# Moving the column-sum fold to VectorE and reordering four instruction queues of an attention kernel

## The reference, cut to what matters

```python
qkv = jnp.einsum('bsh,hf->bsf', x, w_qkv)             # split in q, k, v, 16 heads of 128
scores = jnp.einsum('bhqd,bhkd->bhqk', q, k) / jnp.sqrt(128.)
probs = jax.nn.softmax(scores, axis=-1)
values = jnp.einsum('bhqk,bhkd->bhkd', probs, v)      # k is kept, q is summed
out = jnp.einsum('bsf,fh->bsh', values, w_o)
x = _layernorm(x + out)
```

## Time and profile before

| | us |
|---|---|
| median of three runs | 2747.32 |
| the profiled execution, its own time | 2753.47 |
| its span, first to last instruction | 2751.7 |
| PE busy | 2644.6 (96%) |
| DVE busy | 2170.7 (79%) |
| ACT busy | 1562.8 (57%) |
| POOL busy | 1409.5 (51%) |

### The profile page before, as it was taken

One profiled execution on the slowest core, in us unless ns is written; L12 is line 12 of the kernel. 1 busy time (PEld: TensorE's weight loads), 2 busy tenths in 40 slices (PEclk: granted clock), 3 DMA queues, 4 the chain that ended last, 5 costly groups with the idle time before them and its releaser, 6 DMA issues.

```text
span 2751.7 us, 40658 instructions
## 1 busy us (share of the span) xinstructions
PE 2644.6 (96%) x12450; PEld 2163.3 (79%) x12450; DVE 2170.7 (79%) x3096; ACT 1562.8 (57%) x2627; POOL 1409.5 (51%) x1042
## 2 busy tenths in 40 slices
PE   9999999998999999989999999899999999999998
PEld 7777777777877777777777777777777778888887
DVE  6988888988788888878888888788888787433346
ACT  5655555557666666676556666666655532244434
POOL 3677767545655554556555545555555210266520
PEclk9999999999999999999999999999999999999999
DMA  5455455643533336344343453433334331378954
GB/s 176 146 168 154 150 168 151 220 159 114 181 114 116 112 112 209 110 136 151 107 123 111 121 192 113 168 108 103 104 117 145 101 119 42 107 237 249 260 151 153
DMA packets 351134, 397.51 MB, mean 144 GB/s; under 512 B 132780, under 2 KB 269996, under 8 KB 350496
## 3 DMA queue, kind: packets, MB, share of 16 engines
q1 hardware_dynamic: 340512, 383.92, 44.5%
q0 software_dynamic: 10496, 12.02, 2.4%
HBM read 299.58 MB, written 106.43 MB: 148 GB/s over the span
## 4 chain that ended last, share of the span: by engine, by line
PE 59%; DVE 7%; issue 6%; POOL 2%; ACT 1%; ACTq 0%; DVEq 0%; POOLq 0%
PE banks L2497 17%; PE banks L2568 13%; PE banks L2602 9%; PE banks L2406 5%; PE banks L2455 5%; PE banks L2468 3%; PE banks L2415 2%; DVE colsum L1918 2%; DVE neg_max L1901 1%; PE banks L2578 1%; PE banks L2442 1%; POOL val L948 1%; DVE rows_a L1948 1%; PE banks L2330 1%; POOL qk L957 0%
## 5 line engine op out<-in xcount | busy, mean ns | idle before, releaser
L2568 PE MATMUL banks<-qk 128*128 128x512 f32 x3072 | 786.0, 391 | 21.9 <-POOL qk L957 20.7
L1901 DVE TENSOR_REDUCE neg_max<-banks 128x1 f32<-128x1024 f32 x512 | 624.3, 1220 | 219.6 <-PE banks L2568 217.0
L2497 PE MATMUL banks<-xt,w_all 128*128 128x512 f32 x3024 | 761.4, 394 | 33.6 <-DVE rows_a L1948 12.0
L2497 PEld LDWEIGHTS banks<-xt,w_all 128*128 128x128 f32 x3024 | 565.7, 189 | 179.7 <-DVE rows_a L1948 22.2
L1413 ACT ACTIVATE raws<-banks,neg_max 128x1024 f32<-128x1024 f32 x392 | 438.4, 1118 | 459.8 <-DVE neg_max L1901 456.4
L2568 PEld LDWEIGHTS banks<-qk 128*128 128x128 f32 x3072 | 579.3, 189 | 147.0 <-POOL qk L957 23.3
L1918 DVE SCALAR_TENSOR_TENSOR colsum<-raws,inv,colsum 128x1024 f32<-128x1024 f32 x343 | 535.6, 1562 | 13.5
L2602 PE MATMUL banks<-wo_sb,val 128*128 128x512 f32 x1536 | 385.9, 396 | 16.0 <-POOL wo_sb L898 14.4
L2602 PEld LDWEIGHTS banks<-wo_sb,val 128*128 128x128 f32 x1536 | 292.2, 191 | 82.5 <-issue 19.0
L944 POOL TENSOR_TENSOR folded<-folded,colsum 64x1024 f32<-64x1024 f32 x49 | 116.9, 2385 | 376.3 <-ACT folded L1384 376.3
L2484 PE MATMUL banks<-xt,w_all 128*128 128x512 f32 x1152 | 279.4, 392 | 6.4 <-DVE xt L2117 6.4
(11 more groups left out here) (233 smaller groups left out, 3421.0 us busy)
## 6 DMA issues: line engine op xcount, KB each, us to landing
w_all<-w_jobs SPq DMA_DIRECT2D x144, 512.0 KB
w_all<-w_jobs SPq DMA_DIRECT2D x72, 768.0 KB
w_jobs<-xt SPq DMA_DIRECT2D x96, 256.0 KB, 3.5
x_jobs<-xt SPq DMA_DIRECT2D x48, 448.0 KB, 5.5
xt<-x_jobs SPq DMA_DIRECT2D x21, 1024.0 KB, 10.8
w_jobs<-w_all SPq DMA_DIRECT2D x72, 256.0 KB, 3.3
wo_raw<-in_w_o SPq DMA_DIRECT2D x63, 256.0 KB, 2.9
raws<-in_w_qkv SPq DMA_DIRECT2D x48, 256.0 KB
```

The costliest lines, as they stand in the source:

```text
L1901: dve.tensor_reduce(neg_max[:, t % 2], p_s[:, t % 2], AX_X, ALU.max, negate=True)\
L2497: ins = pe.matmul(psum[:, bank], w_slot[pos % 7][:, a, c], x[:, half, c], start=(opens and c == 0 and (a, half) == PASSES[0]), stop=(c == ...
L2568: ins = pe.matmul(p_s[:, t % 2, keys], qk[:, par, Q, a, at], qk[:, par, K, b, keys], start=((a, b) == PASSES[0]), stop=((a, b) == PASSES[-1]))
```

## The change

Six edits, none of which adds or removes arithmetic:

1. `fold_cs` of batches 1 to 3 goes from POOL to DVE, in step 1 right behind `max_tile`. POOL's semaphore for it disappears; `hi_cs` and the first `add_tile` of a head wait for DVE's.
2. POOL in batch 0: `lo_cs` stands ahead of `lo_t(n - 1, 1)`, and `lo_wo(n - 1, 1)` ahead of `sum_t(n, 0)`. SP in batch 0: in even slots `load_wo` comes right behind `store_w`.
3. POOL in the first halves: `scale_x` (k = 1) and `lo_x` (k = 0) go to the end of the half.
4. ACT: `copy_v` moves from step 7 to step 6; `evac_u` of P1 from step 1 to step 0 of the second halves of batches 1 to 3.
5. ACT, k = 1: the moments of tiles 0 and 1 of the second set are read later, tile 0 in step 7, tile 1 in step 0 of the second half, along with tile 2 and ahead of `write_x`.
6. PE: the product P3 of the second half is computed behind `spread` rather than ahead of it.

```diff
@@ -631,6 +631,8 @@
         def plain(i, s):
             n = 2 * i + s
             store_w(n + 1)
+            if s == 0 and i > 0:
+                load_wo(n - 1, n - 1, 1)
             if n + 2 < H:
                 load_w(n + 2, n + 2)
             if 2 <= n - 1 <= H - 3:
@@ -639,8 +641,6 @@
                 load_t(n, 0)
             if s == 1:
                 load_wo(n - 1, n - 1, 0)
-            elif i > 0:
-                load_wo(n - 1, n - 1, 1)
             x_step = n == 0 or (s == 1 and i < PB - 1)
             if x_step:
                 load_x(0, i + s, i + s)
@@ -939,10 +939,6 @@
             size = 7 * P if b < B - 1 else KC * P
             pool.tensor_tensor(low, x_own[:, 0:size], rounded(high), ALU.subtract).then_inc(pool_x, 1)
 
-        def fold_cs(m):
-            on_pool.wait_ge(act_cs, 3 * m + 1)
-            pool.tensor_tensor(folded[:], folded[:], colsum[0:HP], ALU.add).then_inc(pool_f, 1)
-
         def lo_val(m, r):
             on_pool.wait_ge(act_val, m + 1)
             pool.tensor_tensor(val2[:, r, LO], val[:, r], rounded(val2[:, r, HI]), ALU.subtract)\
@@ -990,18 +986,18 @@
             if s == 0 and not is_first(i):
                 lo_wo(n - 2, 0)
             late_sums = not isinstance(i, int) or 2 <= n - 1 <= H - 3
+            if not (is_first(i) and s == 0):
+                lo_cs(n - 1)
             if late_sums:
                 lo_t(n - 1, 1)
-            if not (is_first(i) and s == 0):
-                lo_cs(n - 1)
+            if s == 0 and not is_first(i):
+                lo_wo(n - 1, 1)
             if sums:
                 sum_t(n, 0)
             if not end:
                 lo_w(n + 2, Q)
             if x_step:
                 sum_x(0, i + s)
-            if s == 0 and not is_first(i):
-                lo_wo(n - 1, 1)
             if sums:
                 lo_t(n, 0)
             if not end:
@@ -1017,7 +1013,6 @@
             n = 2 * i
             m = n + 1
             at, k1 = k == 0, k == 1
-            fold_cs(n - 1)
             if at and b < B - 1:
                 sum_x(b, T * b)
             lo_cs(n - 1)
@@ -1026,14 +1021,14 @@
             lo_val(n - 2, 0)
             lo_block(m, 1, 1)
             add_v(i, 0)
-            if k1:
-                scale_x(2 * (b - 1))
             lo_val(n - 1, 1)
-            if at:
-                lo_x(b, T * b)
             lo_block(m, 1, 2)
             add_v(i, 1)
             lo_wo(n - 1, 1)
+            if k1:
+                scale_x(2 * (b - 1))
+            if at:
+                lo_x(b, T * b)
 
         def second_half(b, k, i):
             n = 2 * i + 1
@@ -1383,11 +1377,8 @@
             on_act.wait_ge(pool_cs, m)
             act.copy(folded[:], colsum[HP:P]).then_inc(act_cs, 1)
 
-        def hi_cs(m, by_pool=False):
-            if by_pool:
-                on_act.wait_ge(pool_f, m - (H - 3))
-            else:
-                on_act.wait_ge(dve_cs, m + 1)
+        def hi_cs(m):
+            on_act.wait_ge(dve_cs, m + 1)
             on_act.wait_ge(pe_cs, 2 * m)
             act.copy(cs[0:HP], folded[:]).then_inc(act_cs, 1)
@@ -1458,7 +1449,7 @@
                     if k1:
                         read_x(c, [0, 1])
                 if t == 2:
-                    hi_cs(n - 1, True)
+                    hi_cs(n - 1)
                     hi_upper_cs(n - 1)
                     if k1:
                         read_x(c, [2])
@@ -1471,7 +1462,6 @@
                     hi_val(n - 2, 0, i)
                     if k1:
                         read_x(c, [3])
-                        read_x(c + 1, [0])
                 if t == 5:
                     evac_v(i, 3)
                     hi_block(i, 0, m, 1, 1)
@@ -1483,10 +1473,9 @@
                     hi_block(i, 0, m, 1, 2)
                     hi_block(i, 0, m, 1, 3)
                     hi_wo(n - 1, 1, i)
-                if t == 7:
                     copy_v(i)
-                    if k1:
-                        read_x(c + 1, [1])
+                if t == 7 and k1:
+                    read_x(c + 1, [0])
                 exp_tile(n, t, ex_late)
 
         def second_half(b, k, i):
@@ -1496,13 +1485,17 @@
             c = 2 * (b - 1)
             for t in range(T):
                 if t == 0:
+                    if k1:
+                        read_x(c + 1, [1, 2])
+                    if b > 0:
+                        evac_u(i, AT_S1 + P1, m, 0)
                     upper_cs(n - 1)
                     if k1:
-                        read_x(c + 1, [2])
                         write_x(c, [0, 1])
                 if t == 1:
-                    evac_u(i, AT_S1 + P1, m, 0)
-                    if not (b == 0):
+                    if b == 0:
+                        evac_u(i, AT_S1 + P1, m, 0)
+                    else:
                         evac_v(i, 5)
                     if k1:
                         read_x(c + 1, [3])
@@ -1901,17 +1894,14 @@
             dve.tensor_reduce(neg_max[:, t % 2], p_s[:, t % 2], AX_X, ALU.max, negate=True)\
                 .then_inc(dve_m, 1)
 
-        def add_tile(n, t, of, by_pool=True):
+        def add_tile(n, t, of):
 
             tau = n * T + t
             on_dve.wait_ge(act_e, tau + 1)
             dve.reciprocal(inv[:, t % 2], rowsum[:, t % 2]).then_inc(dve_r, 1)
             on_dve.wait_ge(dve_r, tau + 1)
             if t == 0:
-                if by_pool:
-                    on_dve.wait_ge(pool_f, n - (H - 2))
-                else:
-                    on_dve.wait_ge(dve_cs, n)
+                on_dve.wait_ge(dve_cs, n)
                 dve.tensor_scalar(colsum[:], of[:, 0], inv[:, 0], None, ALU.mult).then_inc(dve_p, 1)
             else:
                 on_dve.wait_ge(dve_p, tau)
@@ -2016,7 +2006,7 @@
                     if t == 5:
                         lo_val(n - 1, 1)
                 if t >= 1:
-                    add_tile(n, t - 1, ex, False)
+                    add_tile(n, t - 1, ex)
 
         def first_half(b, i):
             n = 2 * i
@@ -2037,6 +2027,8 @@
                 if t == 5:
                     add_block(i, 0, m, 2)
                 max_tile(n, t)
+                if t == 1:
+                    fold_cs(n - 1)
                 if t == 3:
                     times_v(0 if eighth else b, n - 1, 1, i - 1)
                 if t == 4:
@@ -2578,7 +2573,7 @@
                 pe.matmul(p_o[:, half], ones[:], cs[:, at], start=True, stop=True).then_inc(pe_cs, 1)
 
         def spread_last():
-            on_pe.wait_ge(dve_cs, H - 1)
+            on_pe.wait_ge(dve_cs, M)
             for half in range(HALVES):
                 at = slice(half * NB, half * NB + NB)
                 for part, of in ((HI, cs[:]), (LO, last_lo)):
@@ -2648,7 +2643,7 @@
             of = b + 1 if end else b
             for t in range(T):
                 scores(n, 1, t, True)
-                for j in {0: (P1, P2), 1: (P7, P6), 2: (P4, P5), 3: (P3,)}.get(t, ()):
+                for j in {0: (P1, P2), 1: (P7, P6), 2: (P4, P5)}.get(t, ()):
                     qk_unit(of, i, 1, j)
                 if t == SPREAD:
                     if seventh:
@@ -2657,6 +2652,7 @@
                         on_pe.wait_ge(act_ve, evacs(i, 6))
                     on_pe.wait_ge(dve_qc, 3 * (2 * i + 2 - H) + 1)
                     spread(n - 1)
+                    qk_unit(of, i, 1, P3)
                 if t in (4, 5):
                     v_early(of, i, t - 4)
                 if t >= 4:
```

2 lines of the change are left out of this document (1 added, 1 removed).

## The result

The changed kernel takes 2769.97 us, the median of five runs (2767.57 to 2778.45), the kernel before 2750.27 in five runs beside it (2746.57 to 2754.33). The ratio is 1.0068, its 95% interval 1.0054 to 1.0083. The forecast was 2743 with a range of 2712 to 2765. The spans of the two profiled executions are 2768.3 and 2751.7 us.

What follows compares the result with a forecast made beforehand. The PE, busy 96% of the span, was taken as the bound, with batch 0 pairs set by the weight sums' chain. Terms +19.1 - 24.9 - 2.6 + 3.8 = -4.6 gave 2743 us from the median, range 2712 to 2765.

Steps and rivals of the forecast that it cites:

- The chain: Batch 0: the weight sums' four links, not the PE, set the pair's 73.94 us; lengthened, heads 2 to 14 lose +19.1.
- its new link of 23.2 us: Batch 0, last link of a pair: with lo_cs ahead of lo_t it takes 23.2 us, against 16.2.
- rival A: Batch 0: the chain has slack, pairs fall towards 69.0 us; 2690 to 2725, chance 0.24.
- The 1.8 us between 72.2 and 73.94: Batch 0: difference between the four summed links and the measured pair, said to be the PE's own stalls.
- POOL loses twice that, nobody waits for it there: Middle pairs of batches 1 to 3: DVE gets 2.4 us more a pair, POOL loses twice that, without anyone waiting.
- the -0.85 us for each odd slot: Odd middle slots, 17 of them: gaps at P6 and P3 go, with other small waits; -14.5 us in all.
- The signs that the prediction named: In middle pairs no PE gap at P6 and none at copy_v, pairs of about 63 us.
- Rival C: Odd middle slots: DVE's fold becomes the bound at 1848 ns, the gain of 14.5 us goes; 2757, chance 0.07.
- k = 1 and k = 0: First and second halves of these pairs: k = 1 -22.6 and +20.0 us, k = 0 -4.4 and +8.2 us.
- The 40.7 us for the half: k = 1 second half: write_x waits for scale_x, delaying exponentials and P4; +6.7 us each, three times +20.0.
- Rival B: Chain at 78.2 us a pair, k = 1 second half +9, middle pairs winning only 10.4; 2753 to 2770, chance 0.21.
- Rival D: Whole kernel: only an order changes, gains and losses both small; 2747, no change, chance 0.10.

Runs made afterwards that it cites:

- The odd swap alone: Kernel before with one edit: POOL in odd slots of batch 0 does lo_cs ahead of lo_t(n - 1, 1); 2784.08 us, ratio 1.0111.
- its undoing: Changed kernel with POOL in odd slots of batch 0 doing lo_t(n - 1, 1) ahead of lo_cs again; 2738.47 us, ratio 0.9954.
- the last kernel: Changed kernel, lo_t before lo_cs (odd slots), add_v after lo_cs, units before store, load_t before store_t, k = 1 scale_x early, ACT work spread; 2687.67 us.

## Why the prediction was wrong

**Batch 0 was right in its mechanism, and its size is in part luck.** The chain, its new link of 23.2 us (23.8 measured in the pair that it was read from, 24.4 on average), the shorter third link (13.3, measured 13.2), the pair of 77.2 (77.3), and where the PE would wait instead: for exponentials behind `hi_t`. The odd swap alone and its undoing show the cause from both sides. The last link came out 1.2 us above its forecast on average, and the first shrank by 1.1, which was not forecast; the two cancel. And the argument against rival A, that the links add up to the measured pair, was empty, because they always do. The 1.8 us between 72.2 and 73.94 are not the PE's own stalls either: the same four links take 71.8 to 74.5 us from pair to pair, and the prediction had read one of the short ones.

**The step that failed is in the middle pairs: "POOL loses twice that, nobody waits for it there", and with it the -0.85 us for each odd slot.** The measured change is +0.55 us in each of the 17 slots. I looked for who waits for POOL, and found nobody. I did not ask when POOL's next instruction would then start, and beside what. Taking the fold out let `add_v` start some 5 us earlier in the slot, onto DVE's `add_tile`, and 0.85 us of DVE at that point is 0.74 of the slot. The experiment that moves only `add_v` takes 12.6 of the 23.9 us back. The remainder is in the two terms that I had priced from the idle times: with `add_v` out of the way an odd slot takes 31.9 us, 0.2 less than before and not 0.85. `evac_u` a step earlier still helps, but the PE runs into the next wait, 0.72 us at P3 for `add_block`, which I had charged with nothing because `spread` and a score tile lie between. P3 ahead of `spread` costs 0.41 a slot more, so that edit is good, only smaller than the gap. The signs that the prediction named say the same: P6 still waited 0.42 us, and a middle pair takes 64.4 us (31.8 + 32.6) as before and not 63.

There is a second part to it, which moving `add_v` leaves in place. In the odd middle slots that `add_tile` ended 4.53 us into the slot before the change, ends 5.98 after it and 5.15 with `add_v` moved (medians of the 17). Of the 1.45, 0.83 is the collision. The other 0.6 is about what the even slot gained: the PE reaches the odd head that much sooner and DVE does not. That the lead is lost again in this way is how I read the traces; no run tests it.

**Rival C had the right rule and the wrong victim.** It expected DVE's fold to be held up; the 63 folds were not. What was held up is `add_tile`, which reads two tiles of SBUF while `add_v` reads two. That is what the Trainium skill's page "SBUF — State Buffer", section "Who interferes with whom", says of any such pair, and the trace agrees: 1.28 us alone, 2.13 beside `add_v`. It was cited for the instruction that the change adds, when it should have been applied to each pair that the change brings together.

**k = 1 and k = 0 were right in mechanism and near in size, with slips in the working**: +16.8 for +20.0, +10.5 for +8.2, -23.1 for -22.6, -6.1 for -4.4. In k = 1 both causes were named, the wait for `scale_x` and ACT's reads and writes behind it, but as one wait at P4; measured were two, 4.04 us at the third score tile and 2.00 at P4. Relieving the first is worth 2.3 us a slot, and ACT's order together with an earlier `scale_x` the larger part. The 40.7 us for the half do not follow from the terms printed beside them (34.13 - 1.9 + 7.2 + 2.5 = 41.9), and 39.2 to 39.9 were measured. In k = 0 the load of the units went out 11.1 us into head 33 (1168.88, the head starting at 1157.74), 8.0 later than before. The prediction says 4.0, though its own rows give about 7 (the store at 4.8 and the load 5.4 behind it); P5 started at 15.7 and not at 14.3.

**Rival A fell**, since the pairs of batch 0 did not shorten. **Rival B**, whose 2753 to 2770 holds the measured time, hit it by luck: none of its three causes came. Its chain was 78.2 us a pair (77.3 measured), its k = 1 second half +9 (+5.6), and its middle pairs were to lose only the 14.5 of the odd slots, where these lost 9.4 on top. **Rival D**, no change, is out at +0.68%.

**What stays open**: how the larger part of the k = 1 second half divides between `scale_x`'s place and ACT's order, and whether `evac_u` a step earlier helps or costs there. Why `lo_t` behind `lo_cs` runs 3.46 us in place of 2.40 the traces show in part: in the odd slots 5 to 13 of the changed kernel it starts while an `add_tile` still has 1.2 us to run, and takes 3.45 to 3.46; where no `add_tile` was running at its start it took 2.1 to 2.4 in this trace. No run moved one of the two.

## What to carry to other kernels

Taking an instruction off an engine moves everything behind it forward; ask of each what it will now run beside, not only who waits for it. In a chain of rounds through several engines, measure the links over several periods and ask what each waits for. Their sum equals the period in any case, so it proves nothing; change one link and see. Here 6.8 us put into one link cost 4.6 us a pair, the other links giving some of it back, and the idle time of POOL was no cover. When a wait for one engine is removed, look at what else stands in the same queue ahead of the next thing that the bound engine needs: it can give the price back.

## What the runs showed of the hardware

**VectorE beside GpSimd.** `add_tile`, a VectorE operation on two fp32 tiles of 128 x 1024 in SBUF, takes 1.28 us where GpSimd is idle, and 2.12 to 2.24 us in the odd middle slots where it starts soon after a GpSimd operation on tiles of 128 x 512. In the rows above, only the later of two loses time. `lo_wo`, started 0.13 us ahead of an `add_tile`, keeps its 1.28 us, and that `add_tile` takes 2.24. `add_v`, started while that `add_tile` runs, takes 2.27 in place of 1.31, and the `add_tile` behind it, started while `add_v` runs, takes 2.13. So one collision is handed on to the next operation.

**The clock behind a wait.** In head 51 of the changed kernel the PE was idle for 4.04 us, and then six matmuls took 2.93 us in place of 1.52. The granted clock of the 2 us from 1762 on was 0.50, that is 1.2 GHz:

```profile
1762.00:1764.00 2.00, 1.99 (x5) 0.99 (x3) 0.00 (x0) 1.97 (x6) 0.00 (x0) 0.50 0.00 0
```

The mean over this half of 39.87 us was 0.91, and 1.00 in the same half of the last kernel (33.55 us), where no wait was over 1 us. So in a kernel bound by TensorE a wait can cost more than its length. The length alone did not tell: behind a wait of 3.27 us in one run twelve matmuls took 3.02 us, behind one of 3.26 us in another they took 5.49, in place of 2.88.
